# Routed experts of an adaLN mixture-of-experts network: gate and up products as three float32r products

## What is computed

```python
logits = flat @ gate_W.T                      # 8 experts
top_v, top_i = top_k(softmax(logits), 2)
g = silu(einsum('td,edf->etf', flat, w1_e))   # 128 -> 512, each routed expert
u = einsum('td,edf->etf', flat, w3_e)         # 128 -> 512
out_e = einsum('etf,efd->etd', g * u, w2_e)   # 512 -> 128
routed = einsum('te,etd->td', gates, out_e)
shared = einsum('nbsf,nfd->bsd', gs * us, w2_s) / 8   # all tokens, 512 wide in all
return 0.5 * shared + 0.5 * routed
```

## Time and profile before

| | |
|---|---|
| median of 3 runs | 2394.73 us (2389.87 to 2395.68) |
| the profiled execution, its own time | 2396.32 us |
| its span | 2394.5 us |
| busy: PE, PEld, DVE, ACT, POOL | 95%, 56%, 73%, 54%, 57% of the span |
| attention and all that is before the shared units | about 0 to 2015 us |
| shared units and scatter | about 2015 to 2120 us |
| loop over tiles | about 2128 to 2366 us |

### The profile page before, as it was taken

The page is one execution under the profiler, slowest core; times in us unless marked ns, Lnnn a source line. Parts: engine busy times, 40 slices in busy tenths (PEclk is TensorE's granted clock), DMA queues, the critical chain, the costliest instruction groups (busy, mean ns, idle before and its releaser), DMA issues.

```text
span 2394.5 us, 39749 instructions
## 1 busy us (share of the span) xinstructions
PE 2279.8 (95%) x10734; PEld 1346.7 (56%) x10735; DVE 1745.4 (73%) x4469; ACT 1284.8 (54%) x1712; POOL 1371.4 (57%) x743
## 2 busy tenths in 40 slices
PE   4999999899999999999999999999999999989995
PEld 2566566456555555656555555656555554546663
DVE  5687885687777777787777777787777777844444
ACT  0323323466666666666666666666666663324442
POOL 2121120477777677767777676767777677633231
PEclk7999999999999999999999999999999999989998
DMA  7002202000000000000000000000000000311114
GB/s 285 1 1 82 82 1 99 16 16 11 13 10 12 22 11 13 10 15 11 22 10 12 13 11 13 10 24 11 13 10 12 13 8 11 147 42 43 43 41 130
DMA packets 70273, 80.84 MB, mean 34 GB/s; under 512 B 17940, under 2 KB 56084, under 8 KB 70040
## 3 DMA queue, kind: packets, MB, share of 16 engines
q1 hardware_dynamic: 65848, 70.99, 9.4%
q0 software_dynamic: 4352, 8.99, 1.1%
HBM read 49.38 MB, written 32.66 MB: 34 GB/s over the span
## 4 chain that ended last, share of the span: by engine, by line
PE 88%; DVE 5%; POOL 2%; issue 1%; DMA 1%; SPq 1%; ACT 1%; POOLq 0%; DVEq 0%; ACTq 0%
PE P L1832 19%; PE P L1796 12%; PE P L1817 10%; PE P L1818 10%; PE P L1762 5%; PE P L2210 3%; PE P L1942 3%; PE P L2214 3%; PE P L2233 3%; PE P L1839 3%; PE P L1747 2%; PE P L1850 2%; PE P L1928 2%; PE P L1801 2%; PE P L1990 1%
## 5 line engine op out<-in xcount | busy, mean ns | idle before, releaser
L1464 ACT ACTIVATE big<-P 128x1024 f32<-128x1024 f32 x512 | 512.1, 1020 | 200.5 <-PE P L1818 84.0
L947 DVE CUSTOM_DVE_ANT_0 big<-P,near 128x512 f32<-128x512 f32 x512 | 348.6, 681 | 235.4 <-PE P L1796 232.8
L1832 PE MATMUL P<-big,V 128*64 128x512 f32 x2048 | 483.4, 603 | 0.3 <-ACT big L1470 0.3
L600 POOL TENSOR_TENSOR spair<-spair,big 128x1024 f32<-128x1024 f32 x192 | 457.9, 2385 | 14.0
L600 POOL TENSOR_TENSOR opair<-opair,big 128x1024 f32<-128x1024 f32 x192 | 456.3, 2377 | 14.3
L1796 PE MATMUL P<-Ka,Qa 96*128 96x512 f32 x1008 | 441.0, 458 | 2.9 <-DVE Kb L935 1.4
L950 DVE TENSOR_REDUCE mhalf<-P 128x1 f32<-128x512 f32 x512 | 349.0, 682 | 84.5 <-PE P L1796 73.6
L1817 PE MATMUL P<-Qa,Ka 97*128 97x512 f32 x1024 | 408.8, 399 | 1.2 <-ACT big L1464 1.1
L1818 PE MATMUL P<-Qb,Kb 128*128 128x512 f32 x1024 | 406.1, 397 | 0.0
L1796 PEld LDWEIGHTS P<-Ka,Qa 96*128 96x128 f32 x1008 | 181.4, 190 | 216.0 <-issue 117.7
L587 POOL TENSOR_TENSOR big<-big,sinv 128x512 f32<-128x512 f32 x64 | 82.4, 1287 | 375.4 <-DVE sinv L921 375.4
(11 more groups left out here) (303 smaller groups left out, 3505.5 us busy)
## 6 DMA issues: line engine op xcount, KB each, us to landing
slots<-later SPq DMA_DIRECT2D x4, 4224.0 KB, 14.5
Ka<-auxrows SPq DMA_DIRECT2D x64, 128.0 KB, 2.2
big<-in_wex SPq DMA_DIRECT2D x8, 768.0 KB, 10.6
xt<-slots SPq DMA_DIRECT2D x76, 66.0 KB, 1.8
wqk<-in_whead SPq DMA_DIRECT2D x64, 64.0 KB, 1.8
near<-in_aux SPq DMA_DIRECT2D x64, 64.0 KB, 1.8
big<-yrows SPq DMA_DIRECT2D x8, 512.0 KB, 7.2
xs<-in_x SPq DMA_DIRECT2D x4, 512.0 KB, 11.6
```

What stands on the lines that cost most here:

```text
L600: pool.tensor_tensor(psum8[s][:, :], psum8[s][:, :], pfull[:, j % RING, :], ALU.add).then_inc(S["p_added"], 1)
L947: dve.tensor_tensor_reduce(waste, P[:, bank, :], near[s][:, left:left + HALF], -1.0, 3.0e38, ALU.add, ALU.min, mhalf[:, i, t:t + 1]).then_ ...
L1464: act.activation(pfull[:, j, :], banks(2 * (j % 2)), ACT.Exp, scale=DH1 ** -0.5).then_inc(S["exp_done"], 1)
L1832: mm = pe.matmul(P[64 * i:64 * i + 64, 4, :], V1[:, j, s, :], half(pfull[:, j, :], i), start=(j == 0), stop=(j == T - 1))
```

## The change

The routed experts' gate and up products are no longer plain float32 products. Weights and turned tiles are parted into a high part (rounded to float32r) and a low part (what the rounding left), and each product becomes three float32r products that add up in PSUM: high tile by high weights, high tile by low weights, low tile by high weights. The product of the two low parts is left out.

- **Weights.** ACT writes the high parts of w1 and w3 of each expert (128x1024) to `whi` (`weights_high`), which lies where the attention's `Ka`, `Kb`, `Qa`, `Qb` were (now one tensor, `kq`), behind units 4 to 7 of batch 2 and 0 to 3 of batch 3; the first one waits for the weights' DMAs. DVE subtracts them from `wexp` in place (`weights_low`), between units 3 and 7 of batch 3 and once behind unit 7.
- **Tiles.** ACT's copy goes to `xhi` (rounded), and a new DVE instruction writes `xlo` = PSUM - `xhi` (`tile_low`). PE's two waits for ACT's copy become waits for this instruction.
- **Products.** `tile_up` has six matmuls where it had two. The down products, the shared expert's and all else stay as they were.

```diff
@@ (DVE, ACT: the weights) @@
+            def weights_low(e):
+                dve.wait_ge(E["w_hi"], e + 1)
+                dve.tensor_tensor(wexp[:, e, 0:2 * F1].bitcast(F32R), wexp[:, e, 0:2 * F1], whi[:, e, :].bitcast(F32), ALU.subtract).then_inc(E["w_lo"], 1)
+            def weights_high(e):
+                if e == 0:
+                    act.wait_ge(G["we_in"], 16 * E1)
+                act.activation(whi[:, e, :], wexp[:, e, 0:2 * F1], ACT.Copy).then_inc(E["w_hi"], 1)
...
+                    if b == B - 2 and u > 3 or b == B - 1 and u < 4:
+                        weights_high((u + 4) % E1)
@@ (DVE, ACT: the tiles) @@
+            def tile_low(r, j, kr):
+                k = r * GROUP + j
+                dve.wait_ge(E["t_T"], kr(k + 1))
+                dve.sem_inc(G["passed"], 1)
+                dve.tensor_tensor(xlo[:, j % 4, :], P[:, 5, 0:128], xhi[:, j % 4, :].bitcast(F32), ALU.subtract).then_inc(E["t_lo"], 1)
...
             for j in range(GROUP):
+                tile_low(0, 3 + j, same)
                 tile_gu(0, 1 + j, same)
                 tile_out(0, j, same)
                 tile_dest(0, 2 + j, same)
...
-                act.activation(xT[:, j % 4, :], P[:, 5, 0:128], ACT.Copy).then_inc(E["t_T"], 1)
+                act.activation(xhi[:, j % 4, :], P[:, 5, 0:128], ACT.Copy).then_inc(E["t_T"], 1)
@@ (PE) @@
-                    pe.wait_ge(E["t_T"], kr(k))
+                    pe.wait_ge(E["t_lo"], kr(k))
                 pe.transpose(P[:, 5, 0:128], xt[:, j % XBUF, 2:2 + D], identf[:, :]).then_inc(E["t_turned"], 1)
...
-                pe.wait_ge(E["t_T"], kr(k + 1))
+                pe.wait_ge(E["t_lo"], kr(k + 1))
+                def up(bank, at):
+                    pe.matmul(P[:, bank, :], xhi[:, j % 4, :], whi[:, e, at], start=True, stop=False)
+                    pe.matmul(P[:, bank, :], xhi[:, j % 4, :], wexp[:, e, at].bitcast(F32R), start=False, stop=False)
+                    return pe.matmul(P[:, bank, :], xlo[:, j % 4, :], whi[:, e, at], start=False, stop=True)
...
-                pe.matmul(P[:, i, :], xT[:, j % 4, :], wexp[:, e, 0:F1], start=True, stop=True).then_inc(E["t_w1"], 1)
+                up(i, slice(0, F1)).then_inc(E["t_w1"], 1)
...
-                pe.matmul(P[:, 2 + i, :], xT[:, j % 4, :], wexp[:, e, F1:2 * F1], start=True, stop=True).then_inc(E["t_w3"], 1)
+                up(2 + i, slice(F1, 2 * F1)).then_inc(E["t_w3"], 1)
```

More of the change, by code:

```diff
@@ L197, in network @@
               *(f"t_in{i}" for i in range(XBUF)), *(f"t_out{i}" for i in range(YBUF)), *(f"m_y_in{b}" for b in range(B)))}
-        E = {"t_turned": S["turned"], "t_T": S["hT_act"], "t_w1": S["w1_mm"], "t_w3": S["w3_mm"], "t_silu": S["silu_done"],
+        E = {"w_hi": S["vec_copied"], "w_lo": S["h_free"], "t_lo": S["xd_done"], "t_turned": S["turned"], "t_T": S["hT_act"], "t_w1": S["w1_mm"], "t_w3": S["w3_mm"], "t_silu": S["silu_done"],
              "c_kept": S["ydT_copied"], "t_gate": S["gates"], "t_idx": S["dests"], "t_gu": S["gu_done"], "t_gu_turned": S["yd_turned"], "t_guT": S["hT_dve"],
@@ L253, in network @@
         xt = sb("xt", [128, XBUF, ROW])
-        xT = sb("xT", [128, 4, 128])
+        xhi = sb("xhi", [128, 4, 128], F32R)
+        xlo = sb("xlo", [128, 4, 128], F32R)
         tgate = sb("tgate", [128, YBUF])
@@ L276, in network @@
         wv = sb("wv", [128, 2, DH1])
-        Ka = [sb(f"Ka{s}", [128, N], F32R) for s in range(2)]
-        Kb = [sb(f"Kb{s}", [128, N], F32R) for s in range(2)]
-        Qa = [sb(f"Qa{s}", [128, N], F32R) for s in range(2)]
-        Qb = [sb(f"Qb{s}", [128, N], F32R) for s in range(2)]
+        kq = sb("kq", [128, 8, N], F32R)
+        Ka, Kb, Qa, Qb = ([kq[:, 2 * i + s, :] for s in range(2)] for i in range(4))
+        whi = kq
         V1 = sb("V1", [128, T, 2, DH1])
@@ L1329, in _ @@
                         invert(1, HEADS - 1, c)
+                if not ahead:
+                    weights_low(0)
+                    weights_low(1)
                 unit(b, 4)
@@ L1333, in _ @@
                     route_logits(b + 1)
+                else:
+                    weights_low(2)
+                    weights_low(3)
                 unit(b, 5)
@@ L1336, in _ @@
                     route_probs(b + 1)
+                else:
+                    weights_low(4)
+                    weights_low(5)
                 unit(b, 6)
@@ L1339, in _ @@
                     route_hits(b + 1)
+                else:
+                    weights_low(6)
                 unit(b, 7)
@@ L1342, in _ @@
                     route_slots(b + 1)
+                else:
+                    weights_low(7)
             add_out_of(B - 1)
@@ L1378, in _ @@
             same = lambda v: v
+            tile_low(0, 0, same)
+            tile_low(0, 1, same)
             tile_dest(0, 0, same)
+            tile_low(0, 2, same)
             tile_gu(0, 0, same)
@@ L1387, in _ @@
                 for j in range(GROUP):
+                    tile_low(r, 3 + j, dve.snap)
                     tile_gu(r, 1 + j, dve.snap)
```

## The result

Median **2379.23 us** of 5 runs (lowest 2376.14), against 2394.73 before; the ratio is 0.993, with a 95% interval of 0.9916 to 0.9944. The profiled execution took 2376.14 us, its span is 2374.3 (before 2396.32 and 2394.5).

The account below looks back on a forecast made before the run. PE's list was taken to bound the tile loop, POOL's scatters the time before it. 2396.3 - 22.6 + 1.05 + 2.75 = 2377.5 us; with the profiled execution 1.6 above the median, 2376 us, range 2371 to 2384.

Parts of the forecast that it names:

- The products: PE's gate and up products in the tile loop: each 0.153 us shorter, 148 of them, -22.6 us.
- Rival E: Float32r matmuls with weight load and register address do not hide the load; slower, 2433 us; chance 0.04.
- The low part of a tile: DVE's new instruction in the tile loop: hidden behind PE's 2.85 us step, 0 us, 0.04 to 0.15 to spare.
- the disputed point: On DVE, the multiplication's waits run during the low part, so it starts 0.45 us behind the low part's start.
- B: Rival: the ring through DVE sets the pace, step 2.90 to 2.95 us, 2380 to 2383 us; chance 0.18.
- C: Rival: weight subtractions hold POOL for their whole length, loop starts 11 us later, 2383 us; chance 0.07.
- F: Rival: no change, ring and start both at their worst, step 3.10 us, 2395 us; chance 0.06.
- this ring: Per-tile chain of PE turning, ACT copies, DVE low part and multiplication: 2.70 to 2.81 us against PE's 2.85.
- The start: Work ahead of the tile loop: loop starts 3.8 us later, from the high part on the path and held scatters.
- The high part on the path: One ACT weight copy between Exp and table load delays Silu of unit 6 and the last scatter, +1.05 us.
- Held scatters: POOL's scatters that start inside DVE's weight subtractions take longer, delaying the last one: +2.75 us, bounds 0 and 10.
- Rival D: POOL is not held by the weight subtractions at all; 2373 us; chance 0.09.

Follow-up runs that it names:

- experiment 7: Changed kernel with three extra copies of the tile's low part, four in all, ahead of the multiplication on DVE; 2412.84 us (before 2410.09 on that chip).
- experiment 6: Changed kernel with each tile's low part made twice on DVE, once to a tensor nobody reads; 2393.77 us (before 2407.66 on that chip).
- experiment 1: Changed kernel with DVE's multiplication placed ahead of the next tile's low part; 2370.41 us (before 2393.09 on that chip).
- experiment 5: Changed kernel with one plain float32 product in place of the three float32r ones, output incomplete; 2394.16 us (before 2393.09 on that chip).
- experiment 2: Changed kernel with a body's last turning moved to the head of the next, ahead of the expert-number load; 2377.32 us (before 2393.09).
- experiment 3: Changed kernel with the expert-number load at the body's head and the previous body's last turning behind it; 2387.77 us (before 2407.66).
- experiment 8: Changed kernel without the eight subtractions making the weights' low parts, whole weights used instead; 2390.33 us (before 2407.66 on that chip).
- experiment 9: Changed kernel with the weights' high parts moved so none stands between Exp and table load; 2394.35 us (before 2407.66 on that chip).
- experiment 10: Changed kernel with multiplication first, load then turning at the body's head, and high parts moved; 24 tiles a body; 2372.09 us, ratio 0.9897.
- experiment 11: Changed kernel with multiplication first, load then turning at the body's head, and high parts moved; 12 tiles a body; 2371.94 us, ratio 0.9903.
- experiment 12: Changed kernel with multiplication first, load then turning at the body's head, and high parts moved; 8 tiles a body; 2372.10 us, ratio 0.9902.
- experiment 4: Changed kernel with 12 tiles in the loop body, five ends and 16 numbers a load; 2375.29 us (before 2393.09 on that chip).

## Why the prediction was right, and where it was off

Forecast 2376 us, measured 2379.23 in the median.

**The products: right.** -22.6 us was said for 74 tiles, 21.7 of it for the 71 steps, and -22.9 was measured over these: 0.322 us a step, not 0.306, since a float32r matmul takes 0.232 us and a plain product 0.858. They are that far apart with a weight load and a register address each. Rival E is out. The head of the loop, with the other three tiles, gained 1.3 us where 0.9 was in the sum.

**The low part of a tile: right in steady state, near the lower of my bounds.** 0.04 to 0.15 us to spare were foreseen, and experiment 7 gives 0.06. The 0.06 us between multiplication and weight load in the trace is no second measurement of it: it is as long where PE waits. That the multiplication's waits are worked off in the shadow of the low part, 0.45 behind its start, was the disputed point: it is 0.37, and experiment 6 shows that even a second low part fits there. From the turning to the low part it is 1.55 us (2171.62 to 2173.17) where 1.45 was added up; the two errors all but cancel. B, C and F did not come about.

**Missed: the ends of the loop body.** "Before, this ring did not hold the low part and had 0.3 us or more of room" was written, and then 0 us was charged. The room mattered at two places that the steady state does not show, and the forecast has no term for them: before, PE's load of expert numbers was mostly hidden by it. That is the step that failed. The ends cost **+4.8 us**, not 0. Two parts of it can be told apart. 3.4 us go when the low part no longer stands ahead of the multiplication (experiment 1: 4.6 us at the two ends against 7.95), nearly all of it with the half clock. The other 1.4 us stay even then, and they are also there with long products and the clock at 1.00 (experiment 5). So they are not the price of the low part alone: a shorter step takes the same room away. That the gap is the load of numbers is shown by its own record and by experiments 2 and 3 (it goes where the load goes). An end at which the clock fell costs 3.7 to 4.0 us (eight such ends), one with 24 tiles at which it stayed 1.1 to 2.7.

What makes the clock fall stays open in part. Over the 40 ends of all kernels, the five gaps of 1.98 to 2.06 us in PE were all followed by the half clock, of the eleven of 1.59 to 1.89 us three were (1.60 and twice 1.73), and of the 24 shorter ones none. So it followed the longest gaps each time, and what decides in the middle is not shown: at 1.79 and 1.89 us it stayed up. With the low part first, float32r products, a body of 24 and the load behind the turning (after, experiments 2, 6, 7, 8 and 9) it fell at 8 of 12 ends; with the multiplication first (experiments 1, 10 to 12) at none of 17, but 15 of these gaps are of 1.54 us or less, so the order of DVE's list is not shown to matter beyond the gap. Each kernel has one traced execution.

**The start: the parts right, the sum too large.** +3.8 us was said, +2.0 measured in the profiled execution. The high part on the path: 1.05 said, Silu 0.94 later behind Exp, and the last batch's first scatter 0.74 later. Experiment 9 puts the Silu back; the first turn came 1.7 us earlier in it, more than the part can be worth, so that chip's numbers give the sign and not the size. Held scatters: 2.75 said; 2.36 in the trace of after, 2.80 in experiment 9, and none without subtractions (experiment 8). What I had not counted is that the map of tiles holds scatters as well, and which of them it holds depends on where they stand: three before (1.20, 1.65, 1.68), and with POOL's list 0.74 later one (1.47 at 2101.59), 1.14 us saved. That was the luck of the phase. 0.74 + 2.36 - 1.14 makes the 2.0. Rival D is out.

The Trainium skill ("SBUF — State Buffer", Who interferes with whom) infers that descriptor generation is spared by a DVE instruction with two SBUF inputs. The rows at 2105.90 and 2108.89, and experiments 8 and 9 beside each other, do not bear that out for an indirect DMA: POOL's instruction that starts in such an instruction lasts until some 0.8 us behind its end. Whether it is the descriptors or POOL's reading of the row numbers in SBUF that waits, no run tells.

**The number was partly luck.** The sum made against the profiled execution was 2377.5 us, and that of after took 2376.14, 1.4 us less. The missed 4.8 us at the ends were made up by three others: 1.8 us less at the start, 1.6 more from the products and the head of the loop, and 2.8 us that lie where the change does nothing. From median to median (2394.73 to 2378.2) the gain is 16.5 us, where 18.8 was forecast.

## What to carry to other kernels

Read the ends of a hardware loop's body apart from its steady state: an instruction that a queue hides in every step may be what is late where an engine loads registers, and that gap can be followed by the half clock as well (here behind each of the five longest gaps). When a product gets cheaper, measure what is left between the engines' hand-overs (here 0.06 us of 2.83) before something else goes into that ring; doubling the suspect tells nothing if the second one fits into a wait. Put the work that others wait for first in an engine's list: with the multiplication ahead of the low part the loop was 3.6 us shorter in its one run.

## What the runs showed of the hardware

- PE's load of expert numbers from SBUF into registers takes 1.88 to 2.04 us for 28 numbers (after, experiments 1 and 2), 1.10 to 1.13 for 16 (experiment 4) and 0.85 to 0.97 for 12 (experiment 12), at the ends of the body. In after it starts 0.3 us behind DVE's last multiplication at the first end and 0.6 at the second; to PE's next turn it is 2.44 and 2.71 us (2.46 and 2.85 before), of which only what PE still has to do is hidden.
- A gap of 1.98 to 2.06 us in PE was followed by the half clock (passes 0.42 us apart instead of 0.23) at 5 of 5 ends, one of 1.59 to 1.89 us at 3 of 11, a shorter one at none of 24. At each of the eight the clock stayed down for 3.4 us.
- Three waits and one 0.29 us instruction on DVE cost 0.37 us from start to start; with a second such instruction between, 0.40; with four in all, 0.80.
- An indirect DMA on POOL that starts inside a DVE subtraction of two 128x1024 SBUF inputs (1.22 us) takes 1.30 to 1.89 us instead of 0.96 (after, experiment 9), and none behind the map of tiles does without the subtractions (experiment 8).
